# Seven attentions run the products, sums and norms behind them; VectorE adds the residuals of a four-layer decoder

## What is computed

```python
y = attention(x) @ Wo + bo          # 8, 32 or 64 features in each of the heads
x = layernorm(x + y)                # (v - mean) / sqrt(var + eps), one place with RMS norm
```

## Time and profile before

| | |
|---|---|
| median of 3 runs | 1848.97 us |
| profiled execution, own time | 1849.52 us |
| its span, first to last instruction | 1846.9 us |
| around the span | 2.6 us |
| mean granted TensorE clock | 0.902 of full speed |
| TensorE busy | 1549.2 us (84%) |
| VectorE busy | 1040.8 us (56%) |
| ScalarE busy | 643.8 us (35%) |
| GpSimd busy | 211.0 us (11%) |
| instructions | 22396 |

### The profile page before, as it was taken

How to read it: one execution, slowest core, us unless ns; L and a number is a source line. 1 busy time by engine, 2 the same in 40 slices (tenths; PEclk the granted TensorE clock), 3 DMA queues, 4 the chain that set the end, 5 groups by cost and what they waited for, 6 DMA issues and landing times. The chain is left out here.

```text
span 1846.9 us, 22396 instructions
## 1 busy us (share of the span) xinstructions
PE 1549.2 (84%) x8280; PEld 707.8 (38%) x8280; DVE 1040.8 (56%) x2589; ACT 643.8 (35%) x926; POOL 211.0 (11%) x227
## 2 busy tenths in 40 slices
PE   1798689995677999988989998988988679996986
PEld 0332344442233344446433333353446423344343
DVE  4696445447945677753444962535445457734444
ACT  1366242214324033333424663412221255542431
POOL 2000010001000524331000000000000103321000
PEclk9899689996979889998998997997996789997798
DMA  4000000002000000000020000000010000000000
GB/s 200 0 1 1 1 1 0 1 26 108 1 0 1 17 29 2 1 1 1 1 88 13 1 1 0 1 1 1 1 68 1 1 0 1 2 1 1 1 1 12
DMA packets 4075, 27.16 MB, mean 15 GB/s; under 512 B 384, under 2 KB 2432, under 8 KB 2944
## 3 DMA queue, kind: packets, MB, share of 16 engines
q1 hardware_dynamic: 2912, 25.22, 3.4%
q10 hardware_dynamic: 1056, 0.52, 0.1%
HBM read 25.21 MB, written 0.52 MB: 14 GB/s over the span
## 5 line engine op out<-in xcount | busy, mean ns | idle before, releaser
L792 DVE TENSOR_REDUCE maxima<-banks 128x1 f32<-128x512 f32 (+4 forms) x640 | 362.7, 603 | 103.5 <-PE banks L647 96.4
L929 ACT ACTIVATE big<-banks 128x1024 f32<-128x1024 f32 (+2 forms) x320 | 294.3, 960 | 262.4 <-PE banks L690 94.1
L675 PE MATMUL banks<-big 32*128 32x512 f32 (+6 forms) x1280 | 230.3, 607 | 17.0 <-DVE big L813 12.6
L647 PE MATMUL banks<-big 32*128 32x77 bf16 (+6 forms) x1024 | 157.4, 293 | 22.9 <-ACT big L238 6.1
L1390 DVE TENSOR_TENSOR big<-big,banks 128x512 f32<-128x512 f32 (+1 forms) x116 | 79.7, 687 | 151.5 <-PE banks L1303 146.1
L711 PE MATMUL banks<-big,v_heads 128*9 128x512 f32 (+7 forms) x1024 | 158.6, 565 | 6.3 <-ACT heads_out L852 3.2
L446 POOL TENSOR_TENSOR rstd<-mean_var,minus_half 128x4 f32<-128x4 f32 x34 | 34.5, 1014 | 1078.8 <-DVE mean_var L346 1078.8
L1365 ACT ACTIVATE big<-banks 128x512 f32<-128x512 f32 (+1 forms) x116 | 69.1, 596 | 178.1 <-PE banks L1302 178.0
L647 PEld LDWEIGHTS banks<-big 32*128 32x128 bf16 (+1 forms) x1024 | 57.1, 97 | 177.3 <-DVE maxima L792 90.8
L1333 PE MATMUL banks<-big,moe_weights 128*128 128x512 f32 (+1 forms) x232 | 118.9, 597 | 3.0 <-ACT big L1373 2.6
L336 DVE BATCH_NORM_STATS2 stats<-banks 128x6 f32<-128x128 f32 x128 | 28.5, 284 | 135.6 <-PE banks L324 135.6
(11 more groups left out here) (409 smaller groups left out, 2254.6 us busy)
## 6 DMA issues: line engine op xcount, KB each, us to landing
moe_weights<-in_moe SPq DMA_DIRECT2D x1, 4864.0 KB, 14.9
moe_weights<-in_moe SPq DMA_DIRECT2D x1, 4768.0 KB, 22.0
moe_weights<-in_moe SPq DMA_DIRECT2D x1, 3264.0 KB, 10.5
moe_weights<-in_l3x SPq DMA_DIRECT2D x1, 3072.0 KB, 10.0
late_weights<-in_l2x SPq DMA_DIRECT2D x1, 2048.0 KB, 8.0
moe_weights<-in_l SPq DMA_DIRECT2D x1, 1234.0 KB, 13.1
rows<-in_rows SPq DMA_DIRECT2D x1, 1152.0 KB, 8.0
late_weights<-in_turned SPq DMA_DIRECT2D x1, 1152.0 KB, 17.3
```

Source lines behind the costliest of these rows:

```text
L647: last = nc.tensor.matmul(RING[n % NR][:, x * klen:x * klen + last_key(t)], q[rows, t * P:(t + 1) * P], ks[rows, 0:last_key(t)], start=Tru ...
L675: last = nc.tensor.matmul(SC[pair % 2][0:size, j % 2, n0:S], ks[rows, i * P:i * P + size], q[rows, n0:S], start=True, stop=turned)
L792: nc.vector.tensor_reduce(dst, src, AX_X, ALU.max).then_inc(ring_free.up(), 1)
L929: nc.scalar.activation(E[pair % NEP][0:size, :, n0:S], SC[pair % 2][0:size, :, n0:S], ACT.Exp, scale=scale).then_inc(exp_ready.up(), 1)
```

## The change

The function `norms` becomes a class `Norms` with the same work split into parts that a block can call: `pe_first` (half 0's transposes and product, tile by tile, as a generator), `pe_rest`, `dve_first`, `dve_rest`, `powers` and `act_rest`. Base and bias row no longer go through TensorE. VectorE adds the base to the product of each half out of PSUM and writes the sum to SBUF (`own_sum`, one instruction over four tiles); the bias row is added to the base ahead of that, for both halves in one instruction (`dve_first`). Statistics and norms read this sum in SBUF. The copy of `keep` goes. In layer 3's feed-forward block the transposed base is replaced by three more instructions of VectorE over all eight tiles (`beside`), in the block ahead. Where there is a `Front`, half 0 is now copied out by VectorE and half 1 by ScalarE, and half 1's transposes come after half 0's product. In ten places `norms` stays a block of its own. In the seven behind a `row_attention`, the parts are in the attention's block: `row_attention` has a parameter `finish`, whose parts follow the engines' own programs, and steps of `pe_first` stand between the last rounds. TensorE waits with `heads_done` until VectorE has written the last head of a half. GpSimd's powers follow its own work of the attention, and no transfer of the DMA queues is moved.

```diff
-def norms(c, terms, steps, front=None, weigh=None, keep=None, load=None, store=None):
...
-                for half in range(2):
-                    multiply(half, (True,))
-                for half in range(2):
-                    copied = front_dve if half else front_act
-                    pe.wait_ge(copied.sem, copied.at(1))
-                    multiply(half, (False,)).then_inc(sum_ready.up(), 1)
...
-            for half in range(2 if keep is not None else 0):
-                act.wait_ge(stats_ready.sem, stats_ready.at(half + 1))
-                nc.scalar.copy(keep[:, half * H:(half + 1) * H, :], c.bank[half].rearrange("p (t f) -> p t f", t=H)).then_inc(kept.up(), 1)
...
+def product_of(c, srcT, w, n=1):
+    return lambda t: [(srcT[:, i, t * P:(t + 1) * P], w[:, i * P:(i + 1) * P]) for i in range(n)]
+def turned_back(c, srcT):
+    return product_of(c, srcT.unsqueeze(1), c.ident[:])
...
+    SUM, FRONT, TURNED = (2, 3), (4, 5), (0, 1, 6, 7)
...
+    def source(self, i, t):
+        return (self.steps[i - 1].out if i else self.total)[:, t, :]
...
+    def turn_front(self, pe, half):
+        c = self.c
+        for k, t in enumerate(self.tiles(half)):
+            last = c.nc.tensor.transpose(self.front_bank(half)[:, k * P:(k + 1) * P], self.front.src[:, t, :],
+                                         c.ident_bf[:] if self.front.bf else c.ident[:])
+        last.then_inc(self.front_ready.up(), 1)
+    def add_up(self, pe, half):
+        c = self.c
+        for k, t in enumerate(self.tiles(half)):
+            products = self.product(t)
+            for i, (lhsT, rhs) in enumerate(products):
+                last = c.nc.tensor.matmul(c.bank[self.SUM[half]][:, k * P:(k + 1) * P], lhsT, rhs, start=(i == 0), stop=(i == len(products) - 1))
+            if k == ST - 1:
+                last.then_inc(self.sum_ready.up(), 1)
+            yield
+    def pe_first(self, pe, heads_done=None):
+        if heads_done:
+            heads_done(pe, 0)
+        if self.front:
+            self.turn_front(pe, 0)
+            yield
+            pe.wait_ge(self.front_dve.sem, self.front_dve.at(1))
+        yield from self.add_up(pe, 0)
+    def pe_rest(self, pe, heads_done=None):
+        c, final = self.c, self.final
+        if heads_done:
+            heads_done(pe, 1)
+        if self.front:
+            self.turn_front(pe, 1)
+            pe.wait_ge(self.front_act.sem, self.front_act.at(1))
+        for _ in self.add_up(pe, 1):
+            pass
...
+    def own_sum(self, dve, half):
+        vector, ts = self.c.nc.vector, slice(half * ST, (half + 1) * ST)
+        dve.wait_ge(self.sum_ready.sem, self.sum_ready.at(half + 1))
+        if self.weigh:
+            seq(dve, self.step, self.weigh(dve, self.step, half, self.c.bank[self.SUM[half]]))
+            return
+        base = self.base if self.row is None else self.total
+        psum = self.c.bank[self.SUM[half]].rearrange("p (t f) -> p t f", t=ST)
+        seq(dve, self.step, vector.tensor_tensor(self.total[:, ts, :], psum, base[:, ts, :], ALU.add))
...
+    def dve_first(self, dve):
+        vector = self.c.nc.vector
+        if self.row is not None:
+            seq(dve, self.step, vector.tensor_tensor(self.total[:], self.base[:], self.row.unsqueeze(1).broadcast_to([P, NT, P]), ALU.add))
+        if self.front:
+            dve.wait_ge(self.front_ready.sem, self.front_ready.at(1))
+            vector.tensor_copy(self.front.dst[:, 0:S], self.front_bank(0)[:, 0:S]).then_inc(self.front_dve.up(), 1)
+    def dve_rest(self, dve):
+        c, final, n = self.c, self.final, len(self.steps)
+        vector = c.nc.vector
+        for half in range(2):
+            self.own_sum(dve, half)
+            self.own_stats(dve, 0, half)
...
+    def act_rest(self, act):
+        c, final = self.c, self.final
+        scalar = c.nc.scalar
+        if self.front:
+            act.wait_ge(self.front_ready.sem, self.front_ready.at(2))
+            scalar.copy(self.front.dst[:, S:2 * S], self.front_bank(1)[:, 0:S]).then_inc(self.front_act.up(), 1)
...
+            for _ in own.pe_first(pe):
+                pass
+            own.pe_rest(pe)
+        @block.vector
+        def _(dve):
+            own.dve_first(dve)
+            own.dve_rest(dve)
...
+    finish = finish and finish()
...
+    def heads_done(pe, b):
+        g = (b + 1) * NG // B - 1
+        item = sums_turned[g] if turned else spread[g]
+        pe.wait_ge(ring_free.sem, ring_free.at(item + 1))
...
                 pe.wait_ge(project_free.sem, project_free.at(len(projections)))
+            product = finish.pe_first(pe, heads_done) if finish else iter(())
             for r in range(R + later):
...
+                if r == R or r == R + 1 and added_up or r > R and summed(r - turn_after) is not None:
+                    next(product, None)
+            if finish:
+                for _ in product:
+                    pass
+                finish.pe_rest(pe, heads_done)
...
+            if finish:
+                finish.act_rest(act)
...
+                if finish and r == R:
+                    finish.dve_first(dve)
+            if finish:
+                finish.dve_rest(dve)
...
+            if finish:
+                finish.powers(pool)
...
-    attention_8(c, [SK], 8.0 ** -0.5, projections=projections, needs=needs)
-    bias = [] if bo is None else [row_term(c, bo)]
-    norms(c, [natural_term(c, c.X)] + bias + [product_term(c, c.yT8, wo)], [norm], front=Front(c.Y8, c.yT8[:, 0]))
+    attention_8(c, [SK], 8.0 ** -0.5, projections=projections, needs=needs,
+                finish=lambda: Norms(c, product_of(c, c.yT8, wo), [norm], c.X, row=bo, front=Front(c.Y8, c.yT8[:, 0])))
...
+                  finish=lambda: Norms(c, product_of(c, y, c.m("wo"), 8), [Norm(c.XN, eps=1e-6, rms=True, turned=[(hT, c.col("L1_ffn_g2"), None)])],
+                                       c.X))
...
-    norms(c, terms + [product_term(c, h, w2, 4)], steps)
+    norms(c, product_of(c, h, w2, 4), steps, total, total=total)
...
-    norms(c, [natural_term(c, c.X), row_term(c, c.row("L3_attn_b_out")), product_term(c, c.yT8, c.m("L3_woutT"))],
-          [Norm(c.XN, turned=[(x1T, c.col("L3_attn_gamma"), c.col("L3_attn_beta"))])], front=Front(c.Y8, c.yT8[:, 0]))
+    norms(c, product_of(c, c.yT8, c.m("L3_woutT")), [Norm(c.XN, turned=[(x1T, c.col("L3_attn_gamma"), c.col("L3_attn_beta"))])],
+          c.X, row=c.row("L3_attn_b_out"), front=Front(c.Y8, c.yT8[:, 0]))
+    every = lambda name: c.row(name).unsqueeze(1).broadcast_to([P, NT, P])
     def beside(dve, step):
-        nc.vector.tensor_tensor(c.total[:], c.X[:], c.row("L3_attn_beta").unsqueeze(1).broadcast_to([P, NT, P]), ALU.add)
+        seq(dve, step, nc.vector.tensor_tensor(c.XN[:], c.XN[:], every("L3_attn_gamma"), ALU.mult))
+        seq(dve, step, nc.vector.tensor_tensor(c.XN[:], c.XN[:], every("L3_attn_beta"), ALU.add))
+        nc.vector.tensor_tensor(c.XN[:], c.XN[:], every("L3_attn_b2"), ALU.add)
+        nc.vector.tensor_tensor(c.total[:], c.X[:], every("L3_attn_beta"), ALU.add)
```

384 lines of the change are left out of this document (170 added, 214 removed).

## The result

The changed kernel takes 1804.69 us, the median of 4 runs (1803.29 to 1805.44), beside 1848.54 us for the kernel before (1846.86 to 1850.07). The ratio is 0.9762 with an interval of 0.9745 to 0.9779. The forecast was 1804.6. The profiled execution took 1804.04 us of its own, with a span of 1802.1 us, where the sum of the prediction gave 1805.1.

What follows compares the result with a forecast made beforehand. VectorE's statistics waiting on TensorE's products was taken as the bound. Terms 9 + 8.8 + 26.6 = 44.4 us took the profiled 1849.52 us to 1805.1, the median to 1804.6; range 1794 to 1819.

Steps and rivals of the forecast that it cites:

- What bounds it: In the 17 sums and norms, VectorE's first statistics wait 135.6 us for TensorE's last product; TensorE savings there move the end.
- The three with heads of 8: Layer 0's and 1's cross attention and layer 2's attention: gains 1.9, 2.5 and 3.6, with 0.27 each 8.8 us.
- The four with wider heads: Layer 1's causal attention 7.4, layer 2's cross attention 6.9, a1 6.5, a2 4.8; with 1.0 for SBUF, 26.6 us.
- its first sign of being wrong: The forecast would be wrong if the granted clock falls in the attention drains or for longer behind them; no size.
- the warm value of 7.0: Gain at a1's attention if the clock is warm, 7.0 us, against 5.3 cold; 6.5 was taken.
- The ten blocks: The ten places where sum and norm stay blocks: 7.9 us, plus 1.3 from SBUF at five of them, 9 us.
- 1.2 between 0.6 and 1.9: Gain taken for layer 3's attention, with front, row and partly half clock, where half 0's copy waits for the row add.
- SBUF for the norms: Eight norm tiles take 2.36 us from SBUF, 2.63 from PSUM: 0.27 gained except at layer 0's first; no doubled rate.
- Half gain: Seven attention drains: TensorE falls to 1.2 GHz or tiles delay the drain; 13 to 24 us lost, about 1820; chance 0.13.
- The products don't move in effect: Ring or copy holds half 0's product until the drain is over: gain only 26 us, 1823; chance 0.05.
- Slower: TensorE's idle before the first transposes grows 0.7 us, keeping the next stage's start at low clock: 1856 us; chance 0.02.
- the argument against: Against the case of a slower kernel: the next stages' stretches are low already, so the gap before them did its harm.

Runs made afterwards that it cites:

- a filler in layer 3's attention: Changed kernel plus two unused 512-column products between half 0's transposes and the wait for VectorE's copy, only in the norm behind layer 3's attention: 1798.87 us.
- The filled gap: Changed kernel plus unused TensorE products, three behind the last product and one behind the last transposes, in the 16 places that transpose normed tiles: 1779.72 us.
- the shifted kernel: Changed kernel with three unneeded VectorE copies, about 1.9 us, in a block ahead of the first stage, so all work starts later: 1808.88 us.

## Why the prediction was right, and where not

- **What bounds it.** Right. The wait for the product went to half, and the end moved with it.
- **The three with heads of 8.** 8.8 forecast, 8.8 measured. The late last head of layer 1's cross attention, 1.4 us in the prediction for row add, copy and tile together, is the row add nearly alone: with it taken away 1.3 us came back, the copy and the tile staying where they were.
- **The four with wider heads.** 26.6 forecast, 26.4 measured; single ones off by up to 1.0. The one that is off by 1.0 is a2, 4.1 for 5.1, and it is the clock: it fell inside the drain for 3.4 us. Timeline of a2's drain in the changed kernel (line 746 makes the last values, line 882 is the multiplication that ends the heads; cut to its first and last row):

```profile
1732.47 1.06 PE L746 MATMUL banks<-big,v_heads 77*32 77x512 f32 x8 [1.17 <-ACT heads_out L897]
...
1735.84 1.92 PE L332 MATMUL banks<-moe_weights,big 128*128 128x128 f32 x8
...
1738.67 1.06 PE L332 MATMUL banks<-moe_weights,big 128*128 128x128 f32 x8
...
1741.97 0.69 DVE L882 TENSOR_TENSOR big<-big,banks 128x512 f32<-128x512 f32 x1 [0.45 <-PE banks L812]
```

  and in the kernel with a filler in layer 3's attention, which has the same program here:

```profile
1727.47 1.06 PE L748 MATMUL banks<-big,v_heads 77*32 77x512 f32 x8 [1.17 <-ACT heads_out L899]
...
1735.96 0.69 DVE L884 TENSOR_TENSOR big<-big,banks 128x512 f32<-128x512 f32 x1 [0.64 <-PE banks L814]
```

  In the changed kernel the first tile takes 1.92 us and the next 1.06, and from the start of the values to the start of the last head's multiplication it is 9.50 us; in the other kernel 8.49, and a2 gains 5.1 there, what was forecast. Set against the times of the kernel before, the last head is written at 1781.2 and 1780.2, where the prediction had 1780.5, and half 1's statistics start at 1785.9 and 1784.9, where it had 1784.9. So ring, row add and tiles were priced rightly in sum, and the forecast had no term for a fall of the clock inside the drain, though it was its first sign of being wrong. In a1 the opposite: the warm value of 7.0 was the better one, 7.3 came.
- **The ten blocks.** 9 forecast, 8.1 measured. The mis-sized term is layer 3's attention, "1.2 between 0.6 and 1.9": with the 0.27 of SBUF 0.6 measured for 1.5, so 0.3 without it, below the stated range. The reason that I gave for its lower end, that half 0's copy waits for the row add, was nearly free:

```profile
1403.23 1.08 PE L323 MATMUL banks<-ident,big 128*128 128x128 f32 x4 [1.13 <-PEq L2034]
1403.24 1.23 DVE L431 TENSOR_TENSOR total<-x,rows 128x1024 f32<-128x1024 f32 x1 [0.30 <-PEq L2034]
1404.50 0.69 DVE L434 COPY big<-banks 128x512 f32<-128x512 f32 x1
1405.24 2.08 PE L332 MATMUL banks<-moe_weights,big 128*128 128x128 f32 x8 [0.92 <-DVE big L434]
...
1408.85 2.08 PE L332 MATMUL banks<-moe_weights,big 128*128 128x128 f32 x8 [0.68 <-ACT big L477]
```

  The half-clock transposes (1.08) take nearly as long as the add (1.23). What cost is that both products are at 1.2 GHz: 2.08 us each for the 1.16 of half 1's in the kernel with fillers there. In the kernel before, the clock rose 34.1 us after it fell, in the records of base and bias row; here it stayed low for 47.8.
- **SBUF for the norms.** The 0.27 was right for a place, and its ground was not. The prediction read "no doubling" into a row that holds a wait for the second power; a tile does gain 62 ns.
- **What it held for nothing.** The stretches between the places. They came to +1.5 us as a sum of terms from -2.2 to +2.8, about as many of each sign; the first, -1.4, lies ahead of the first norm, where nothing was changed. That the total agreed with the forecast to 0.1 us is therefore luck of this size: the places alone were 1.2 below the forecast, and "between" 1.5 above. The profiled executions alone, 1804.04 for the 1805.1 worked out, are 1.1 apart.
- **The rivals.** *Half gain*: did not happen in six of the seven; a2 shows it in small, 1.0 us of 5.1. *The products don't move in effect*: with them in place but behind the drain, the kernel takes 1820.63, so standing half 0's product, copy and row add in the drain is worth 15.9 us. *Slower*: the stretch behind layer 2's norm was 17.1 us for 20.5, and the time at 1.2 GHz 368 for 362, so these rows show no sign that the 0.7 us that the add puts into the gap cost anything, as the argument against had it: the gap had done its harm before. The add's part of the gap was not tried by itself. The filled gap showed how much harm in the changed kernel: 25 us. The kernel before was not run with fillers. The prediction used the mechanism as a danger only and did not name it as a reserve.

## What to carry to other kernels

Where an engine's first work on a result waits for TensorE, take additive terms off TensorE and let the waiting engine add them; put the half of the product that is ready early between the steps of the pipeline's drain, and test the order, since the same adds in plain blocks gave less than half as much (20.9 us of 44.4). Then look at the gap in which TensorE has nothing to do ahead of a stage that it bounds, and at the granted clock behind it: unused products in that gap were worth as much here as the change's adds (25 us). Compare variants place by place, at places where the clock is the same in both: totals within 4 us of one another may differ only by where the clock rises, and executions of one kernel, the one before, by up to 8.

## What was not expected of the hardware

- The low stretches are long, and end late though TensorE is busy: 47.8 us with 39.7 busy, and 27.3 in the shifted kernel with its last 10.2 wholly busy, where the same work 1.8 us earlier had 17.1.
- 128 unneeded records of 512 columns took 25 us off the total (1779.72 for 1804.69).
- GpSimd's 2.34 us add of 128x1024 fp32 did not lengthen the rows of VectorE that ran wholly beside it: a copy out of PSUM of 0.69 us in layer 3's attention took 0.69 there. Only three such instructions lay beside the six adds.
- Reading PSUM costs a 128x128 norm tile 62 ns, but an add of 128x512 takes 0.692 us with one operand in PSUM (line 380) and 0.692 with both in SBUF (line 1231 of the kernel before).
